# Weights of the second attention and of the experts, split into halves during the first attention

## The reference, cut to what matters

```python
xn = layernorm(x)
x = x + mla_attention(xn) + binarised_ffn(xn)     # 16 heads of 64, rope, softmax over 512 keys
xn = layernorm(x)
x = x + linear_attention(xn) + moe(xn)

# linear_attention: q, k = elu(x @ Wq.T) + 1, elu(x @ Wk.T) + 1; v = x @ Wv.T; causal sums of k v; @ Wo.T
# moe: gate = softmax(x @ Wg + bg); for each of 8 experts, on the tokens that chose it (top 2):
#      y = relu(x @ W1[e] + b1[e]) @ W2[e] + b2[e]          W1 256 x 1024, W2 1024 x 256
```

## Time and profile before

| what | us |
|---|---|
| timed, median of 3 (lowest, highest) | 2285.13 (2284.41, 2285.27) |
| profiled execution: its own time | 2287.67 |
| profiled execution: span, first to last instruction | 2286.0 |
| TensorE busy | 1932.8 (85%) |
| VectorE busy | 1297.8 (57%) |
| ScalarE busy | 894.2 (39%) |
| GpSimd busy | 1330.3 (58%) |
| mean granted TensorE clock | 0.931 |

### The profile page before, as it was taken

The page is one execution under the profiler, slowest core; times in us unless marked ns, Lnnn a source line. Parts: engine busy times, 40 slices in busy tenths (PEclk is TensorE's granted clock), DMA queues, the critical chain, the costliest instruction groups (busy, mean ns, idle before and its releaser), DMA issues. The chain is left out here.

```text
span 2286.0 us, 35324 instructions
## 1 busy us (share of the span) xinstructions
PE 1932.8 (85%) x12804; PEld 1339.6 (59%) x12804; DVE 1297.8 (57%) x1857; ACT 894.2 (39%) x1536; POOL 1330.3 (58%) x860
## 2 busy tenths in 40 slices
PE   5877559999999999999999837777775699999798
PEld 4666424454544445454545435656554699898698
DVE  6666436656666565666576425655544466566343
ACT  4555224434434343434344304232221255555354
POOL 2333238877878786878787614344444366666633
PEclk9888769999999999999999968888887799999899
DMA  3111321323232222313232240121212433324122
GB/s 103 71 73 55 121 69 44 77 47 87 53 93 56 77 63 65 75 39 94 45 93 47 56 142 22 51 60 50 61 49 64 162 84 80 75 43 117 29 43 43
DMA packets 81606, 158.63 MB, mean 69 GB/s; under 512 B 14496, under 2 KB 63520, under 8 KB 75552
## 3 DMA queue, kind: packets, MB, share of 16 engines
q1 hardware_dynamic: 66464, 133.40, 21.1%
q0 software_dynamic: 14592, 18.40, 4.8%
q10 hardware_dynamic: 432, 5.24, 0.6%
HBM read 80.84 MB, written 44.17 MB: 55 GB/s over the span
## 5 line engine op out<-in xcount | busy, mean ns | idle before, releaser
L916 ACT ACTIVATE a_pr<-a_pT 128x1024 f32<-128x1024 f32 x256 | 262.0, 1024 | 428.1 <-PE a_pT L739 428.1
L949 POOL TENSOR_TENSOR a_total<-a_total,a_pr 128x1024 f32<-128x1024 f32 x128 | 321.9, 2515 | 148.1 <-ACT a_pr L916 147.5
L821 DVE TENSOR_REDUCE a_row_max<-a_pG 128x2 f32<-128x1024 f32 x256 | 309.1, 1220 | 149.5 <-PE a_pG L713 149.3
L1825 DVE TENSOR_TENSOR c_h_lo<-c_h,c_h_hi 128x256 fp32r<-128x256 f32 x288 | 213.6, 759 | 196.1 <-ACT c_h_hi L1804 178.5
L752 PE MATMUL a_pA<-a_pr,a_v 128*64 128x512 f32 x1024 | 277.1, 619 | 0.1
L1804 ACT ACTIVATE c_h<-c_pU,c_b_c 128x256 f32<-128x256 f32 x288 | 138.6, 481 | 233.7 <-PE c_pU L103 232.4
L949 POOL TENSOR_TENSOR a_total<-a_pr 128x1024 f32<-128x1024 f32 x64 | 151.8, 2372 | 57.2 <-ACT a_pr L916 57.0
L930 POOL TENSOR_TENSOR a_by_cos<-a_by_cos,a_swapped 128x1024 f32<-128x1024 f32 x64 | 155.7, 2433 | 46.7 <-DMA a_swapped<-a_by_sin 46.7
L937 POOL TENSOR_TENSOR a_qk_lo<-a_by_cos,a_qk_hi 128x1024 fp32r<-128x1024 f32 x64 | 157.8, 2466 | 2.3 <-ACT a_qk_hi L886 2.3
L815 DVE TENSOR_TENSOR a_by_sin<-a_pG,a_sin 128x1024 f32<-128x1024 f32 x64 | 78.4, 1225 | 139.2 <-PE a_pG L103 134.4
L1861 POOL DMA_INDIRECT out_x<-c_y,c_ids x72 | 114.8, 1595 | 41.2 <-DVE c_y L1833 21.8
(11 more groups left out here) (248 smaller groups left out, 5091.1 us busy)
## 6 DMA issues: line engine op xcount, KB each, us to landing
a_swapped<-a_by_sin SPq DMA_DIRECT2D x256, 128.0 KB, 2.3
a_inv_by_head<-mid_inverses SPq DMA_DIRECT2D x32, 512.0 KB, 6.1
c_x_t<-mid_rows SPq DMA_DIRECT2D x37, 272.0 KB
mid_latents<-f_c_parts SPq DMA_DIRECT2D x8, 1024.0 KB, 3.9
a_latent_parts<-mid_latents SPq DMA_DIRECT2D x8, 1024.0 KB, 7.1
d_raw<-in_weights SPq DMA_DIRECT2D x3, 2048.0 KB, 9.1
c_raw<-in_weights SPq DMA_DIRECT2D x3, 2048.0 KB, 8.1
f_x_t<-in_x SPq DMA_DIRECT2D x8, 512.0 KB, 3.8
```

Source lines behind the costliest of these rows:

```text
L821: nc.vector.reduce_max(row_max[:, u % 2, :, t], pair[:], AX.X).then_inc(read, 1)
L916: nc.scalar.activation(pr[:, n % RP, :, :], pT[:], ACT.Exp, scale=SCALE).then_inc(exp_done, 1)
L949: nc.gpsimd.tensor_tensor(total[:, u % 2, :, :], before, pr[:, n % RP, :, :], ALU.add).then_inc(summed, 1)
L1825: nc.vector.tensor_tensor(h_lo[:, m % RH, :], h[:, m % RH, :], h_hi[:, m % RH, :], ALU.subtract).then_inc(h_lo_done[m % RH], 1)
```

## The change

The splits move into stage A. The eight experts' weights (4096 columns each, four chunks of 1024) and the second attention's (1552 columns, two chunks) make 34 chunks. Chunk k belongs to unit 64 k // 34: units 0, 1, 3, 5, ... 15, then 16, 18, ... 32, then 33, 35, ... 47, then 48, 50, ... 62. In such a unit SyncE, after everything else of the unit, stores the halves of chunk k-1 to HBM and loads chunk k; ScalarE casts it after the exponential of t = 2; VectorE subtracts at the unit's end. There is one buffer for the chunk and one for its two halves. B and C then load halves, twice the bytes, instead of raw weights; all splits in B and C go, C holds four sets of weights instead of three, ScalarE issues all their loads in C (after b2's, which before came behind expert 1's), W1 of expert 0 is loaded at B's start and W2 near its end. The two spare copies in HBM are removed.

```diff
@@ stage_a @@
+        for e in range(NE):
+            for layer in range(2):
+                for i in range(WL // CHUNK):
+                    cols = slice(i * CHUNK, (i + 1) * CHUNK)
+                    chunks.append((weights[e * P:(e + 1) * P, layer * WL + i * CHUNK:layer * WL + (i + 1) * CHUNK],
+                                   experts[e * P:(e + 1) * P, layer, :, cols], CHUNK))
+        for at in range(0, W1L, CHUNK):
+            n = min(CHUNK, W1L - at)
+            chunks.append((l1_w[:, at:at + n], l1_split[:, :, at:at + n], n))
+        chunk_of = {k * UNITS // len(chunks): k for k in range(len(chunks))}
...
+                def load_chunk(k):
+                    if k >= 1:
+                        sp.wait_ge(chunk_lo, k)
+                        _, to, n = chunks[k - 1]
+                        sp.dma_start(to, halves[:, :, 0:n].bitcast(F32)).then_inc(chunk_out, 16)
+                    if k < len(chunks):
+                        src, _, n = chunks[k]
+                        sp.dma_start(chunk[:, 0:n], src).then_inc(chunk_in, 16)
...
                     if p == NP - 3 and b + 1 < B:
                         latents_for(b + 1)
+                    if u in chunk_of:
+                        load_chunk(chunk_of[u])
+                load_chunk(len(chunks))
                 spread(UNITS // GROUP - 1)
                 store(B - 1)
                 sp.wait_ge(stored, 16 * B)
-                sp.dma_start(tokens(x1, B), tokens(x1, 0)).then_inc(spare_done, 16)
-                sp.wait_ge(spare_done, 16)
+                sp.wait_ge(chunk_out, 16 * len(chunks))
...
+                def chunk_low(k):
+                    dve.wait_ge(chunk_hi, k + 1)
+                    n = chunks[k][2]
+                    nc.vector.tensor_tensor(halves[:, 1, 0:n], chunk[:, 0:n], halves[:, 0, 0:n],
+                                            ALU.subtract).then_inc(chunk_lo, 1)
...
                     if g >= 0 and u % GROUP in (1, 2):
                         normalise(2 * g + u % GROUP - 1)
+                    if u in chunk_of:
+                        chunk_low(chunk_of[u])
...
+                def chunk_high(k):
+                    act.wait_ge(chunk_in, 16 * (k + 1))
+                    if k >= 1:
+                        act.wait_ge(chunk_out, 16 * k)
+                    n = chunks[k][2]
+                    nc.scalar.copy(halves[:, 0, 0:n], chunk[:, 0:n]).then_inc(chunk_hi, 1)
...
                             values(*values_at(u, t))
+                        if t == NT - 2 and u in chunk_of:
+                            chunk_high(chunk_of[u])
                         if t == NT - 1 and u + 2 < UNITS:
                             qk_high(u + 2)
@@ stage_b @@
-                for n, (src, _) in names.items():
-                    sp.dma_start(raw[n][:], src).then_inc(loaded, 16)
+                sp.dma_start(halves[:].bitcast(F32), l1_split).then_inc(halves_in, 16)
...
-                sp.dma_start(dispatch.raw[:], weights[0:P, :]).then_inc(dispatched, 16)
+                sp.dma_start(dispatch.w1[:].bitcast(F32), experts[0:P, 0, :, :]).then_inc(dispatched, 16)
...
+                            sp.dma_start(dispatch.w2[:].bitcast(F32), experts[0:P, 1, :, :]).then_inc(dispatched, 16)
                             end_experts()
@@ stage_c @@
-        RW = 3
+        RW = 4
...
                     if e:
-                        pe.wait_ge(splits, e)
+                        pe.wait_ge(w_in[w], 32 * (e // RW + (w > 0)))
...
+                def load_weights(e):
+                    if e >= RW:
+                        act.wait_ge(experts_done, e - RW + 1)
+                    act.dma_start(w1[e % RW][:].bitcast(F32), experts[e * P:(e + 1) * P, 0, :, :]).then_inc(w_in[e % RW], 16)
+                    act.dma_start(w2[e % RW][:].bitcast(F32), experts[e * P:(e + 1) * P, 1, :, :]).then_inc(w_in[e % RW], 16)
+
                 x_high()
-                load_weights(nc.scalar, 1)
                 act.dma_start(b2_row[:], b2).then_inc(b2_in, 16)
-                load_weights(nc.scalar, 2)
+                load_weights(1)
                 act.wait_ge(b1_in, 16)
                 for e in range(NE):
+                    if e + 2 < NE:
+                        load_weights(e + 2)
                     with act.Fori(0, tiles_of(act, e)):
...
                     with pool.Fori(0, tiles_of(pool, e)) as i:
                         load_ids(row_of(e, i))
-                        if ahead:
-                            split_high(e + 2, (i % CHUNKS) * CHUNK)
                         send()
-                        if ahead:
-                            split_low(e + 2, (i % CHUNKS) * CHUNK)
                         settle()
```

More of the change, by code:

```diff
@@ L461, with stage_a @@
 GROUP = 4
-def stage_a(nc, wq_t, wk_t, wv_t, wo_t, rope_c, rope_s, neg_blocks_d, ident_d, part, latents, inverses, x1):
+def stage_a(nc, wq_t, wk_t, wv_t, wo_t, rope_c, rope_s, neg_blocks_d, ident_d, part, latents, inverses, x1,
+            weights, l1_w, experts, l1_split):
     with ExitStack() as ctx:
@@ L563, in stage_a @@
         att = sb("att", [P, RA, S])
+        chunk = sb("chunk", [P, CHUNK])
+        halves = sb("halves", [P, 2, CHUNK], F32R)
         pT = st.bank("pT", (P, 2, S))
@@ L1691, in stage_c @@
         b2_in = sem("b2_in")
-        raw_in = [sem(f"raw_in{i}") for i in range(RW)]
-        w_step = sem("w_step")
-        splits = sem("splits")
+        w_in = [sem(f"w_in{i}") for i in range(RW)]
+        experts_done = sem("experts_done")
         x_in = sem("x_in")
@@ L1984, in __init__ @@
             self.own = early.enter_context(nc.sbuf_tensor("d_own", [P, 2, NC1, 2, S], F32))
[L1985 to L1990 removed]
+        self.w2 = sb("w2", [P, 2, WL], F32R)
+        self.spare = sb("spare", [P, 2, WL])
+SCRATCH = {"part": (T, D), "x1": (T, D), "latents": (B * P, 4 * S), "inverses": (2, 2, GROUP, S),
+           "dens": (2, 4, 4 * S), "invs": (2, 4, 4 * S), "rows": (NE * CAP, DW),
+           "experts": (NE * P, 2, 2, WL), "l1_split": (P, 2, W1L)}
 def program(nc, aps):
@@ L1997, in program @@
     stage_f(nc, *of("x w1_rows w1_t w2_t b1 b2 wd_t ln_sb ident_d part latents"))
-    stage_a(nc, *of("wq_t wk_t wv_t wo_t rope_c rope_s neg_blocks ident_d part latents inverses x1"))
+    stage_a(nc, *of("wq_t wk_t wv_t wo_t rope_c rope_s neg_blocks ident_d part latents inverses x1 "
+                    "weights l1_w experts l1_split"))
     with ExitStack() as ctx:
         dispatch = Dispatch(nc, ctx)
-        stage_b(nc, *of("l1_wq l1_wk l1_wvg l1_wo bg own2_d causal_d blocks_d before_d ident_d lower_d ids starts "
-                        "thresholds weights x1 out dens invs rows"), dispatch)
-        stage_c(nc, *of("weights e_b1 e_b2 rows out"), dispatch)
+        stage_b(nc, *of("l1_split l1_wo bg own2_d causal_d blocks_d before_d ident_d lower_d ids starts "
+                        "thresholds experts x1 out dens invs rows"), dispatch)
+        stage_c(nc, *of("experts e_b1 e_b2 rows out"), dispatch)
 def kernel(**inputs):
```

123 lines of the change are left out of this document (35 added, 88 removed).

## The result

The changed kernel takes 2567.5 us (median of 4 runs, 2565.5 to 2570.9), the kernel before 2285.2 beside it: ratio 1.1232, 95% interval 1.1211 to 1.1253. The forecast was 2454, its range 2375 to 2515: the measured time lies 52 us above the range. The direction and the mechanism of the waits were right, and several terms were too small or missing: +282 us where the sum said +169.

The account below looks back on a forecast made before the run. It took TensorE as the bound, losing time where nothing is queued beside a wait, with stage A's exponential ring on ScalarE. +228 - 10 - 2 + 1 - 48 = +169 us on the median 2285.13 gave 2454 us, range 2375 to 2515.

Parts of the forecast that it names:

- Nine long waits: Stage A units that also spread inverses: ScalarE waits for a chunk loaded behind the broadcasts, 16.1 or 17.0 us late each.
- Given back in the next unit: Stage A, unit after a long wait: broadcasts already through, so 4.1 us back, or 1.5 after units like 16.
- Seven middle waits: Stage A units 22, 30, 54 (x1 store, x_t reload) and 5, 13, 37, 45 (latents ahead): 6 us each, 42.
- Seven short waits: Stage A units 18, 26, 50, 58 and 9, 33, 41: chunk lands late, 3.3 us each, 23.
- All other units: Rest of stage A: units 3, 11, 35, 43 hidden by the output projection at 0, the rest together 4 us.
- Port: Stage A: VectorE's subtraction slows GpSimd by 1.0 us per meeting, could cost 34 us, taken as 5.
- Clock: Stage A: TensorE resumes at half speed after waits; 18 us for the nine long ones, 11 for 14 others.
- Spare copies: Two removed HBM copies, each waited for, 6.1 and 4.2 us with the wake-up: -10 us.
- the contention: Stage C: 4 to 8 MB of weights in flight may hold a token tile, +3 us (0 to +12).
- 1 (the chunks hide): Stage A: loads land before ScalarE comes, stage costs 5 to 10 us more, kernel faster at 2234 us; chance 6%.
- Rival 2: Stage A: half of each long wait is won back as other engines run ahead, 63 us less, 2391 us; chance 9%.
- Rival 3: Stage A: port and clock cost their most (+29, +14), no time given back (+24), 2521 us; chance 4%.

Follow-up runs that it names:

- k2: Changed kernel with TensorE running matmuls nobody reads in all of the waits (nine long, seven middle, eight short); ratio 1.1083.
- a0: The changed kernel run again with no edit, base of the second lot; 2569.7 us, ratio 1.1256.
- n1: Changed kernel with VectorE subtracting for the first chunk only (output not the reference's), all chunk waits kept; ratio 1.1241.
- e1: Changed kernel with SyncE issuing the chunk's store and load ahead of the spread of inverses, not behind it; ratio 1.0573.
- n2: Changed kernel with two tiles of halves, the chunk's load issued ahead of the previous chunk's store in the same unit; ratio 1.0942.
- e4: Changed kernel with two buffers, chunk ahead of the spread only in units that have one, subtraction moved to the next unit; ratio 1.0034.
- e3: Changed kernel with the edits of e1 and e2 together: two buffers and the chunk ahead of the spread; ratio 1.0158.
- s1: Kernel before the change without its two spare copies at the ends of stages F and A; ratio 0.9955.
- n3: From e4: experts' halves in HBM in 512-column pieces, subtraction moved only for units 1 and 2 of each four; 2246.8 us, ratio 0.9812.
- e2: Changed kernel with two chunk tiles and two tiles of halves, each chunk loaded one chunk ahead; ratio 1.0188.
- c1: Changed kernel with each stage C weight load on ScalarE's queue cut into four of 512 columns; 2552.3 us, ratio 1.1162.
- k1: Changed kernel with TensorE running 64 matmuls nobody reads in each of the nine long waits; ratio 1.1277.

## Where the prediction was right and where it was too small

Sums over units, each unit from one copy of `a_att` on ScalarE to the next, minus the same in the kernel before. k2 has the waits at full clock, a0 has them as they are.

| Term of the sum | Forecast | k2 | a0 |
|---|---|---|---|
| Nine long waits, themselves | 149 | 149.1 | 166.0 |
| Given back in the next unit | -24 | -7.0 | -4.8 |
| Seven middle waits | 42 | 54.4 | 61.1 |
| Seven short waits | 23 | 31.7 | 37.2 |
| All other units | 4 | 28.6 | 39.1 |
| Port | 5 | 0 (n1) | |
| Clock | 29 | | 41.8 (a0 - k2) |
| Stage A | 228 | | 298.6 |

*Long waits: right.* The chain of bytes (broadcasts, store, load) gave 16.1 and 17.0 us; k2 has 16.1 and 17.1 on the mean. That the cause is the place on SyncE, e1 shows; that it is bytes in line, n2.

*Given back: the step failed.* "Net 14.6 x 5 + 12.9 x 4" assumed 1.5 and 4.1 us back per wait. The units behind the long waits with a projection gave 2.2 each (8.6 of 16.4), the others nothing (+1.6 over four; the fifth, 33, has a chunk of its own). 17 us.

*Middle waits: mis-sized.* Units 5, 13, 37, 45 cost 6.4 each, near the 6 taken. Units 22, 30, 54 cost 9.6 and not 6. There SyncE waits for the store of x1, and in the changed kernel 8.07 us pass in unit 22 from the reload's issue (756.10) to the cast (764.17), where the working had 6.6; the reload itself is issued 1.2 us later in the unit than before (8.5 and not 7.3 us after ScalarE's copy of `a_att`). 12 us.

*Short waits: mis-sized.* 4.5 and not 3.3 each. 9 us.

*Other units: the largest miss of stage A.* The forecast put units 3, 11, 35, 43 at 0, as hidden by the output projection, and "the rest together 4", without a reason. Units 11, 35, 43 are hidden; unit 3 belongs to the first block of tokens, which has no projection yet, and cost 3.8. Unit 1 cost 3.0, units 7, 15, 39, 47 1.6 to 2.3 each; and the units behind a wait, which I had at zero, cost 1.1 to 1.7 in 4, 6, 19, 23, 27, 38, 46, 51, 55, 59 and 2.1 in 31. 25 us. What exactly delays those followers at full clock was not tried.

*Port: mis-sized the other way* (0 for 5 in the changed kernel). Where the waits are gone the subtraction is real: 22 us in e4, its own time and its meetings together. In e3's rows a meeting costs GpSimd 1.0 us, as taken, but the subtraction 2.2, and this had no term: it holds up VectorE's next rotation.

*Clock: right where it was priced, and a part left out.* 41.8 for 29. It was priced at the nine long waits (2 us each, 18) and at 0.8 for the fourteen others (11); k2 gained 16.9 at the long waits and 12.2 at the others (5.5 at the short, 6.7 at the middle ones). The rest, 10.5 in the other units and 2.2 in the units behind the long waits, had no term at all.

*Spare copies: right* (s1: 10.4 +- 4 for 10.3). *Stage B: right* (-2 to -3 for -1).

*Stage C: the contention failed.* "4 to 8 MB in flight beside x_t, ids and the scatter may hold a tile: +3 (0 to +12)". It holds seven: 30.5 us of waits (39.3 less the first, 8.8, which the kernel before has too, 8.3), and TensorE at half speed behind them. The rest of -48 stands as a total (its 26 x 0.3 is 7.8 and not 7.5): without the late tiles stage C would be 494.8 - 51 = 443.8 us by the forecast, and n3 has 456.3, of which 12.1 are its own waits for ScalarE. The whole miss in stage C is 38 us. The forecast went by bytes over a stage that moves 103 GB/s on the mean; in the few microseconds that count the DMA is full (420 GB/s), and there the tile's small rows come through late beside rows of 16 KB and in time beside rows of 2 KB.

Together 71 + 38 us, and 4.6 in unit 0, which lies ahead of the table's first copy and had no term: the 113 us that were missing. So the steps that failed are the contention in stage C (38 us), the other units put at 4 (25), the time given back (17), the clock outside the waits (13) and the sizes of the middle and short waits (12 and 9); 5 of port went the other way.

The rivals: 1 (the chunks hide) was decided by the point that the forecast named; e2 and e4 show that it is the better kernel's behaviour and not this one's. Rival 2 (half won back) was wrong, even more than the forecast. Rival 3 (all of port and clock, nothing given back; 2521 us) was the nearest. Little was in fact given back; that its clock (43 us) meets the measured 41.8 is in part luck, since 12.7 of them fell outside the waits it priced, and its port was wrong.

## What to carry to other kernels

Work that is moved into the gaps of a busy stage costs what its place in the queues costs, not its own time: the same 34 chunks made stage A 299 us longer, 146 (e1), 59 (e2), 24 (e4) and 6 (n3), each net of the 4 us of the spare copy. Issue a load one round ahead into a second buffer, ahead of anything on its queue that waits for an engine, and behind a small load that is needed sooner (e3: 4.3 to 5.7 us in the units with latents). Count every late arrival as the wait, plus the half-speed matmuls behind it, plus something in the next round; of time given back afterwards count next to nothing.

When a load in long rows goes into flight, look at the small-row load on another queue that is needed next: shorter rows for the large one cured it here, at the price of the issuing engine's time (14 us for 8 MB at the start of stage C in n3).

## What the runs showed of the hardware that was not expected

- A token tile of 272 KB in rows of 1088 B lands in 2.8 us on the median and in 11.0 to 14.9 us beside weight rows of 16 KB on another queue; beside rows of 2 KB no tile but the stage's first was waited for, with the same 4 MB per expert and the DMA as full (400 and 420 GB/s).
- The issues of 8 MB on ScalarE's queue took 0.45 to 0.70 us each as four with rows of 16 KB, but 16.03 us as sixteen and 14.03 us as eight with rows of 2 KB (c1, n3).
- A granted clock kept full through nine waits did not shorten the stage (k1); kept full through all of them, it gave 41 us (k2).
- The lot on one chip ran stage B in 380 us where those on the three others took 430, with stages A and C the same: 2% of the whole kernel, more than many edits are worth. Why is not known.
